# Attention scores from two fp16 parts on 32-row bands of TensorE, with the operand stacks loaded ahead of the row maxima

## What is computed

```python
q = (x @ Wq.T + bq).reshape(b, s, 16, 8)      # k and v in the same way
attn = jnp.einsum('bqhd,bkhd->bhqk', q, k) / np.sqrt(8)
attn = jax.nn.softmax(attn, axis=-1) * head_mask[None, :, None, None]
out = jnp.einsum('bhqk,bkhd->bqhd', attn, v).reshape(b, s, 128)
x = layernorm(x + out @ Wo.T + bo)
```

## Time and profile before

| | |
|---|---|
| median of 3 timed executions | 702.23 us (700.29 to 702.65) |
| span of the profiled execution | 760.8 us |
| PE busy | 489.5 us (64%) |
| DVE busy | 401.7 us (53%) |
| ACT busy | 307.2 us (40%) |
| POOL busy | 312.9 us (41%) |

### The profile page before, as it was taken

How to read it: one execution, slowest core, us unless ns; L and a number is a source line. 1 busy time by engine, 2 the same in 40 slices (tenths; PEclk the granted TensorE clock), 3 DMA queues, 4 the chain that set the end, 5 groups by cost and what they waited for, 6 DMA issues and landing times. The chain is left out here.

```text
span 760.8 us, 15877 instructions
## 1 busy us (share of the span) xinstructions
PE 489.5 (64%) x5002; PEld 345.1 (45%) x5003; DVE 401.7 (53%) x871; ACT 307.2 (40%) x551; POOL 312.9 (41%) x465
## 2 busy tenths in 40 slices
PE   2577777788776778876840510049959988989400
PEld 1244444455444445543440400049938877777300
DVE  3544545566454556645767200027737867777246
ACT  1044544554454555544634200027724434434115
POOL 7123333223333331321232777710004756666546
PEclk9879989999898998988975655559979989999755
DMA  2333335434443443453221111100092100000074
GB/s 78 95 97 90 87 99 135 115 100 125 114 134 83 135 120 100 120 150 100 65 72 48 50 53 53 53 12 0 0 241 61 32 29 31 31 30 31 16 202 130
DMA packets 86467, 63.05 MB, mean 83 GB/s; under 512 B 10982, under 2 KB 78896, under 8 KB 86432
## 3 DMA queue, kind: packets, MB, share of 16 engines
q1 hardware_dynamic: 81888, 54.13, 26.4%
q0 software_dynamic: 4544, 8.47, 3.4%
HBM read 31.65 MB, written 29.29 MB: 80 GB/s over the span
## 5 line engine op out<-in xcount | busy, mean ns | idle before, releaser
L456 DVE TENSOR_REDUCE row_max<-s_ps 128x2 f32<-128x512 f32 x256 | 163.9, 684 | 163.3 <-PE s_ps L533 162.0
L367 ACT ACTIVATE probs<-st_ps 128x1024 f32<-128x1024 f32 x128 | 129.3, 1024 | 112.9 <-PE st_ps L545 112.7
L533 PE MATMUL s_ps<-k_stack,q_stack 128*128 128x256 bf16 x512 | 109.6, 301 | 89.1 <-DMA k_stack<-k_rows 80.8
L1305 POOL DMA_INDIRECT results<-gated,dest x78 | 95.4, 1223 | 126.5 <-DVE gated L1408 101.8
L545 PE MATMUL st_ps<-q_stack,k_stack 128*128 128x256 bf16 x512 | 105.7, 293 | 1.2 <-ACT probs L367 1.2
L533 PEld LDWEIGHTS s_ps<-k_stack,q_stack 128*128 128x128 bf16 x512 | 39.8, 103 | 140.3 <-issue 60.3
L1379 ACT ACTIVATE hid_r<-h_ps_r,bias 128x256 f32<-128x256 f32 x156 | 61.2, 475 | 95.7 <-PE h_ps_r L901 54.1
L562 PE MATMUL av_ps<-probs,v_aug 128*32 128x256 f32 x1024 | 79.3, 434 | 0.2 <-ACT probs L367 0.2
L885 POOL DMA_INDIRECT slots<-rows,slot_at x64 | 62.1, 970 | 32.0 <-issue 18.9
L299 POOL TENSOR_SCALAR max_parts<-row_max 128x16 bf16<-128x16 f32 x32 | 6.6, 206 | 151.6 <-DVE row_max L456 149.3
L914 PE MATMUL y_ps_r<-w,hid_r 128*128 x312 | 61.0, 223 | 4.0 <-issue 4.0
(11 more groups left out here) (179 smaller groups left out, 1021.4 us busy)
## 6 DMA issues: line engine op xcount, KB each, us to landing
q_stack<-q_rows SPq DMA_DIRECT2D x32, 204.0 KB
k_rows<-qk_parts SPq DMA_DIRECT2D x96, 64.0 KB, 1.7
k_stack<-k_rows SPq DMA_DIRECT2D x32, 192.0 KB
slots<-empty_row SPq DMA_DIRECT2D x6, 780.0 KB, 10.2
expert<-results SPq DMA_DIRECT2D x16, 256.0 KB, 5.1
w_or_slots<-slots SPq DMA_DIRECT2D x3, 1040.0 KB, 12.0
q_rows<-qk_parts SPq DMA_DIRECT2D x16, 192.0 KB, 2.1
w_or_slots<-in_w_fc SPq DMA_DIRECT2D x9, 256.0 KB, 4.3
```

What stands on the lines that cost most here:

```text
L367: nc.scalar.activation(probs[:, p % 4], st_ps[:, p % 2], ACT.Exp, scale=SCORE_SCALE).then_inc(exp_done, 1)
L456: nc.vector.tensor_reduce(row_max[:, h], s1_ps[:, h % 2], AX_X, ALU.max, negate=True).then_inc(max_done, 1)
L533: mm = nc.tensor.matmul(s1_ps[:, h % 2, t], q_stack[:, b.par, h, t * P:(t + 1) * P], k_stack[:, b.par, h], start=True, stop=True)
L1305: nc.gpsimd.indirect_dma_start(out=a["results"][:, :], out_offset=bass.IndirectOffsetOnAxis(ap=dest[:, t.buf, half:half + 1], axis=0), in_ ...
```

## The change

q and k are split into two fp16 parts, so three products of parts give a score, with a contraction of 24 rows a head. The stacks hold four heads in each of four bands of 32 partitions; a matmul now takes a tile of 24 rows (26 for the shifted scores) of one band instead of 128. The maximum is scaled by 1/256 and split in two parts; k_stack is filled with 256 once, in place of ones and zeros, and stays so in the rows behind the 24. The zero rows of q_rows, the memset of q_stack and four DMAs at the start go. A slot now waits for everything first (wait_for_scores, wait_for_shifted) and then takes score and shifted score matmuls in turns; the shifted scores take the heads in the order n ^ 4, so that the two are always on different bands, and the quads follow in the order n ^ 1. In SP's queue the row writes are four DMAs instead of nine, a half of the stacks four instead of two, and load_max four instead of three; the first half of the stacks of `new` is issued ahead of load_max of `now`, the second half behind it.

```diff
@@ -22,7 +23,13 @@
-ROW_MAX = 6 * DH
+TERMS = 3
+BAND = 32
+BANDS = P // BAND
+IN_BAND = HEADS // BANDS
+TERM_ROWS = TERMS * DH
+MAX_PARTS = 2
+MAX_UNIT = 256.0
...
@@ -82,8 +89,8 @@
-        q_rows = nc.dram_tensor("q_rows", [2, ROW_MAX + 3, HEADS, SEQ], BF16, kind="Internal").ap()
-        k_rows = nc.dram_tensor("k_rows", [2, ROW_MAX, HEADS, SEQ], BF16, kind="Internal").ap()
+        q_rows = nc.dram_tensor("q_rows", [2, TERM_ROWS, HEADS, SEQ], F16, kind="Internal").ap()
+        k_rows = nc.dram_tensor("k_rows", [2, TERM_ROWS, HEADS, SEQ], F16, kind="Internal").ap()
@@ -111,15 +116,14 @@
-        qk_rest = sb("qk_rest", [D, 2, SEQ])
-        qk_parts = sb("qk_parts", [D, 2, 2, 3, SEQ], BF16)
-        q_stack = sb("q_stack", [P, 2, HEADS, SEQ], BF16)
-        k_stack = sb("k_stack", [P, 2, HEADS, SEQ], BF16)
+        qk_parts = sb("qk_parts", [D, 2, 2, 2, SEQ], F16)
+        q_stack = sb("q_stack", [P, 2, IN_BAND, SEQ], F16)
+        k_stack = sb("k_stack", [P, 2, IN_BAND, SEQ], F16)
...
@@ -199,29 +202,28 @@
-            sp.wait_ge(consts_made, 4)
-            for par in range(2):
-                sp.dma_start(q_rows[par, ROW_MAX:ROW_MAX + 3], zero_rows[:].unsqueeze(1).to_broadcast([3, HEADS, SEQ])).then_inc(zeros_out, 16)
-                sp.dma_start(k_stack[ROW_MAX:ROW_MAX + 3, par], one_rows[:].unsqueeze(1).to_broadcast([3, HEADS, SEQ])).then_inc(zeros_out, 16)
-            sp.wait_ge(zeros_out, 64)
-                for part in range(3):
-                    rows = HALF * TILES
-                    sp.dma_start(q_stack[ROW_MAX + part:ROW_MAX + part + 1, b.par, half * HALF:(half + 1) * HALF, :]
-                                 .rearrange("o h (t q) -> o (h t) q", t=TILES),
-                                 max_t[part * rows:(part + 1) * rows, half, :]).then_inc(max_in[half], 16)
+                rows = IN_BAND * TILES
+                for part in range(MAX_PARTS):
+                    for k in range(BANDS // 2):
+                        row = (half * (BANDS // 2) + k) * BAND + TERM_ROWS + part
+                        of = (part * (BANDS // 2) + k) * rows
+                        sp.dma_start(q_stack[row:row + 1, b.par].rearrange("o g (t q) -> o (g t) q", t=TILES),
+                                     max_t[of:of + rows, half, :]).then_inc(max_in[half], 16)
-                heads = slice(half * HALF, (half + 1) * HALF)
-                sp.dma_start(q_stack[0:ROW_MAX + 3, b.par, heads], q_rows[b.par, :, heads]).then_inc(stacks_in[b.par][half], 16)
-                sp.dma_start(k_stack[0:ROW_MAX, b.par, heads], k_rows[b.par, :, heads]).then_inc(stacks_in[b.par][half], 16)
+                for band in range(half * (BANDS // 2), (half + 1) * (BANDS // 2)):
+                    rows = slice(band * BAND, band * BAND + TERM_ROWS)
+                    heads = slice(band * IN_BAND, (band + 1) * IN_BAND)
+                    sp.dma_start(q_stack[rows, b.par], q_rows[b.par, :, heads]).then_inc(stacks_in[b.par][half], 16)
+                    sp.dma_start(k_stack[rows, b.par], k_rows[b.par, :, heads]).then_inc(stacks_in[b.par][half], 16)
...
@@ -243,31 +245,26 @@
-                    q_to = q_rows[b.par, 0:ROW_MAX].rearrange("(r d) h t -> (d h) r t", r=6)
-                    k_to = k_rows[b.par].rearrange("(r d) h t -> (d h) r t", r=6)
+                    q_to = q_rows[b.par].rearrange("(r d) h t -> (d h) r t", r=TERMS)
+                    k_to = k_rows[b.par].rearrange("(r d) h t -> (d h) r t", r=TERMS)
-                            sp.wait_ge(stacks_in[b.par][half], 32 * b.half)
-                    sp.wait_ge(qk_split, 4 * b.n + 1)
-                    for r in range(3):
-                        sp.dma_start(k_to[:, r:r + 1], k_part[:, 0:1]).then_inc(rows_out[b.par], 16)
-                    sp.wait_ge(qk_split, 4 * b.n + 3)
-                    for r in range(3, 5):
-                        sp.dma_start(k_to[:, r:r + 1], k_part[:, 1:2]).then_inc(rows_out[b.par], 16)
-                    sp.wait_ge(qk_split, 4 * b.n + 4)
-                    sp.dma_start(q_to[:, 0:3], q_part[:, 0:3]).then_inc(rows_out[b.par], 16)
-                    sp.dma_start(q_to[:, 3:5], q_part[:, 0:2]).then_inc(rows_out[b.par], 16)
-                    sp.dma_start(q_to[:, 5:6], q_part[:, 0:1]).then_inc(rows_out[b.par], 16)
-                    sp.dma_start(k_to[:, 5:6], k_part[:, 2:3]).then_inc(rows_out[b.par], 16)
-                b = Batch(u, c, 1)
-                if b.exists():
-                    load_max(b, 0)
-                b = Batch(u, c, 0)
-                if b.exists():
-                    sp.wait_ge(rows_out[b.par], 144 * (b.half + 1))
-                    load_stacks(b, 0)
-                    load_stacks(b, 1)
+                            sp.wait_ge(stacks_in[b.par][half], 64 * b.half)
+                    sp.wait_ge(qk_split, 2 * b.n + 1)
+                    sp.dma_start(q_to[:, 0:1], q_part[:, 0:1]).then_inc(rows_out[b.par], 16)
+                    sp.dma_start(k_to[:, 2:3], k_part[:, 0:1]).then_inc(rows_out[b.par], 16)
+                    sp.wait_ge(qk_split, 2 * b.n + 2)
+                    sp.dma_start(q_to[:, 1:3], q_part[:, 0:2]).then_inc(rows_out[b.par], 16)
+                    sp.dma_start(k_to[:, 0:2], k_part[:, 0:2]).then_inc(rows_out[b.par], 16)
+                new, now = Batch(u, c, 0), Batch(u, c, 1)
+                if new.exists():
+                    sp.wait_ge(rows_out[new.par], 64 * (new.half + 1))
+                    load_stacks(new, 0)
+                if now.exists():
+                    load_max(now, 0)
+                if new.exists():
+                    load_stacks(new, 1)
...
@@ -275,48 +272,38 @@
-            nc.gpsimd.memset(zero_rows[:], 0.0).then_inc(consts_made, 1)
-            nc.gpsimd.memset(one_rows[:], 1.0).then_inc(consts_made, 1)
...
-            nc.gpsimd.memset(q_stack[:].rearrange("p b h t -> p (b h t)").bitcast(F32), 0.0).then_inc(consts_made, 1)
...
-                    wait_first(pool, rows_out[b.par], 144 * b.half)
+                    wait_first(pool, rows_out[b.par], 64 * b.half)
-                pool.wait_ge(qk_split, 4 * b.n + 1)
-                nc.gpsimd.tensor_tensor(qk_rest[:], qk[:], parts[:, :, 0], ALU.subtract).then_inc(qk_split, 1)
-                wait_first(pool, qk_split, 4 * b.n + 2)
-                nc.gpsimd.tensor_scalar(parts[:, :, 1], qk_rest[:], 1.0, 1.0, ALU.mult, ALU.mult).then_inc(qk_split, 1)
-                pool.wait_ge(qk_split, 4 * b.n + 3)
-                nc.gpsimd.tensor_tensor(parts[:, :, 2], qk_rest[:], parts[:, :, 1], ALU.subtract).then_inc(qk_split, 1)
+                pool.wait_ge(qk_split, 2 * b.n + 1)
+                nc.gpsimd.tensor_tensor(parts[:, :, 1], qk[:], parts[:, :, 0], ALU.subtract).then_inc(qk_split, 1)
...
@@ -521,37 +508,49 @@
-                pe.wait_ge(consts_made, 7)
-            def scores(b, h):
+                pe.wait_ge(consts_made, 4)
+            def band_of(stack, b, h, rows):
+                lo = h // IN_BAND * BAND
+                return stack[lo:lo + rows, b.par, h % IN_BAND]
+            def wait_for_scores(b, h):
-                    pe.wait_ge(stacks_in[b.par][h // HALF], 32 * (b.half + 1))
+                    pe.wait_ge(stacks_in[b.par][h // HALF], 64 * (b.half + 1))
-                for t in range(TILES):
-                    mm = nc.tensor.matmul(s1_ps[:, h % 2, t], q_stack[:, b.par, h, t * P:(t + 1) * P], k_stack[:, b.par, h],
-                                          start=True, stop=True)
-                mm.then_inc(scores_ready, 1)
-            def shifted_scores(b, h):
-                p = h // 2
-                if h % HALF == 0:
-                    pe.wait_ge(max_in[h // HALF], 48 * (b.n + 1))
-                if h % 2 == 0 and (b.since(1) or p >= 2):
+            def scores(b, h, t):
+                mm = nc.tensor.matmul(s1_ps[:, h % 2, t], band_of(q_stack, b, h, TERM_ROWS)[:, t * P:(t + 1) * P],
+                                      band_of(k_stack, b, h, TERM_ROWS), start=True, stop=True)
+                if t == TILES - 1:
+                    mm.then_inc(scores_ready, 1)
+            def wait_for_shifted(b, n):
+                p = n // 2
+                if n % HALF == 0:
+                    pe.wait_ge(max_in[n // HALF], 64 * (b.n + 1))
+                if n % 2 == 0 and (b.since(1) or p >= 2):
-                for t in range(TILES):
-                    mm = nc.tensor.matmul(st_ps[:, p % 2, h % 2, t], k_stack[:, b.par, h, t * P:(t + 1) * P],
-                                          q_stack[:, b.par, h], start=True, stop=True)
-                if h % 2:
+            def shifted_scores(b, n, t):
+                p, h, rows = n // 2, n ^ 4, TERM_ROWS + MAX_PARTS
+                mm = nc.tensor.matmul(st_ps[:, p % 2, n % 2, t], band_of(k_stack, b, h, rows)[:, t * P:(t + 1) * P],
+                                      band_of(q_stack, b, h, rows), start=True, stop=True)
+                if n % 2 and t == TILES - 1:
-            def quad(b, g):
+            def quad(b, n):
```

(73 more changed lines are left out.)

4 lines of the change are left out of this document (2 added, 2 removed).

## The result

The changed kernel takes 657.62 us (median of 4, 650.02 to 659.51) against 701.99 us: a ratio of 0.934, 95% interval 0.928 to 0.940. It is faster by 44 us, where 79 (to 623) were forecast; the range ended at 655.

What follows compares the result with a forecast made beforehand. TensorE's wait for k_stack once a 22.09 us step was taken as the bound. Steps saved 85 us, start and step 1 14, together 99: span 760.8 to 662. Between 611 in proportion and 642, 623 us was chosen, range 598 to 655.

Steps and rivals of the forecast that it cites:

- (d): Score slots on row tiles: a slot's four matmuls take 0.3 us instead of 0.44, taking 0.3 us off a step.
- 16.0 us a step: Attention steps 2 to 15: forecast step time without the stall, against 22.09 us before, 85 us over 14 steps.
- the clock does not stay up: Rival, score slots: matmuls on 24 of 128 rows leave TensorE at 1.2 GHz; 714 us in proportion, chance 0.07.
- changes of shape: TensorE between tile shapes: about 0.1 us a change, 12 more changes a step, 1.2 us.
- first scores at 16: Start of the kernel: first scores near 16 us instead of 25.84, a gain of 9.8 us.
- (a): SP's queue: stacks ahead of the maxima and smaller, 192 KB a half; TensorE's 80.8 us wait for k_stack goes.
- (b): Maxima's rows queued behind the stacks: they land at 17.0, just in time for slot 0 at 17.3; at worst 1.5 us a step.
- The scaling to the median: Profiled span to timed median: the span's ratio of 0.870 applied to 702.23 us gives 611 us.
- the landings: DMA landings: were two thirds of the profiled run's extra 58.6 us there, the gain is 60 and the time 642 us.
- the reordering does nothing: Rival, stack loads: still late because the row writes are late; step near 20.5 us, 669 us, chance 0.09.
- The maxima's rows: Rival, slot 0: late maxima's rows take the stall's place; step of 18.5 us, 643 us in proportion, chance 0.19.

Runs made afterwards that it cites:

- one_band: full_rows with the score matmuls' operands cut to the 24 (26) rows that hold data, one behind another: 793.08 us, ratio 1.128.
- bands64: The changed kernel with two bands of 64 rows instead of four of 32, zeros below the 26 rows of data: 605.95 us, ratio 0.863.
- full_rows: The changed kernel without bands: one head on partitions 0 to 25, zeros below in q_stack, every score matmul on all 128 rows: 611.43 us, ratio 0.869.
- maxima_first: full_rows with SP's old order, the maxima's rows of the first half ahead of both halves of the stacks: 609.54 us, ratio 0.868.
- order_only: The kernel before with only the stacks' first half issued ahead of the maxima's rows: 656.45 us, ratio 0.9325.
- bands64_waits: bands64 with the shifted scores' wait moved behind the slot's first score matmul: 662.11 us, ratio 0.871, where the kernel before took 761.23 us.
- same_band64: bands64 with shifted scores in order n, a slot's four matmuls in one band: 680.56 us, ratio 0.894, where the kernel before took 761.23 us.

## Why the prediction was wrong

**The step that failed is (d), in what it left out**: the 16.0 us a step, priced at full clock, measured 18.87 us on average over six steps, with granted clocks from 0.54 to 1.00. With it failed the chance of the rival "the clock does not stay up". The prediction counted the row tiles' columns and changes of shape, and set the granted clock near 1.00 because before it fell only behind idle time. In the trace of before every matmul names 128 rows, so these rows could say nothing of matmuls on 24. The rival had the mechanism and was given 0.07; what was held against it, that the full-array work keeps coming, didn't help: in one_band it comes in every step too, at half clock. One of its prices holds: 27.6 us a step for half clock without overlap, and one_band takes 28.3. The other, 24 us with overlap, was too high: such a step of the change takes 22.1. The change itself is at half clock for part of the steps and at full clock for the others. Against a step of 15.87 in bands64, 18.87 is 3.0 more, times 14 = 42 us; that is the shortfall in the profiled execution, for bands64 ends attention 339.3 - 294.9 = 44.4 us earlier. The change's median is 7.6 us above its profiled execution, and 44.4 + 7.6 is the 52 us between the medians of the two.

**The sum for full clock was right.** 99 us were forecast; bands64 gains 391.6 - 294.9 = 96.7 by the end of attention. Its parts: first scores at 16, measured 15.62; a step of 16.0, measured 15.6 to 15.9 in the change at full clock and 15.87 in bands64; (a) no wait for k_stack beyond the first; (b) the maxima's rows in time, 2.7 us of waits in all, though their four issues take 2.71 and not 2.4 us; (d) pairs starting together, 0.22 us a slot rather than the 0.3 taken. What side by side running is worth was 0.3 us a step in the sum; full_rows against bands64 gives 16.47 - 15.87 = 0.6, and 5.5 us in time. About the changes of shape the prediction was right too: the quad at 143.51 starts 0.20 us behind the last pair where 0.11 is the rhythm, 0.09 us a change. The Trainium skill, TensorEngine Tiling (Array Packing), Key Properties, cited there, says that changing the tiling mode drains TensorE. The gap of 0.09 us agrees.

**(a) named the queue where size did most.** The place behind the maxima and the 792 KB in one go were treated as one cause. The runs part them: order alone 46 us, smaller stacks alone (maxima_first, which also has the shorter splits and start, and the matmuls in turns) 93, both (full_rows) 91.

**The scaling to the median was wrong.** The trace of before came from an execution 58.6 us slower than the median, and the prediction shared those between a proportion and the landings. They lie behind attention: from the first router matmul to the end it is 760.8 - 391.6 = 369 us there, 648.3 - 339.3 = 309 after the change and 309 in bands64, 308 in order_only, whose later stages are those of the kernel before, while bands64_waits, on the chip with 761 us for the kernel before, has 365. One row of its waits view:

```profile
ACT hid L1213 <- remote: 78.7, 3, 37.3
```

The same wait, 79.0 us, stands in the waits view of before, and none in those of the change and of bands64; what "remote" is, no view says. So the gain was to be subtracted, not scaled or cut: 702.2 - 99 = 603, and bands64 takes 606. The point chosen, 623, was nearer to the result only because two errors had opposite signs: the clock, which the sum left out, costs the change 657.6 - 606 = 52 us, and the unfounded choice had added 20. That part is luck.

Of the rivals, the one in which the reordering does nothing had the nearest number (669) and the wrong cause: order_only gains 46 us by it alone. The maxima's rows never took the stall's place (643).

## What to carry to other kernels

A tile of few rows may cost more than it saves, if TensorE's clock falls with it, as it did here: try the same matmuls with zero rows up to 64 or 128 before choosing the tile; here that won 52 us (64) and 46 us (128). When two cures for one stall come in one change (order and size here), price each alone. And find the place of a gap between a profiled execution and the median, in a stage the change doesn't touch or in one it does, before scaling by it.

## What the runs showed of the hardware

- With the same data, transfers and matmuls, 128 rows a matmul hold 2.4 GHz and 24 to 26 rows one behind another stay at 1.2 GHz through attention (611 and 793 us), while PE is busy all the time. With two 32-row tiles side by side the clock goes up and down, more up when all 32 rows are named (657.6 to 637.1 us). Two 64-row tiles side by side are at full clock but for the start and a stretch near 249 us (605.95 us), and one 64-row tile at a time from 50 us on (same_band64).
- The added rows add nothing to the result (zeros in q_stack against 256 in k_stack) and still keep the clock up. In the kernel before the rows behind the data are zeros in both stacks, and its quads away from a stall take 1.07 us.
- The clock column reads 1.00 for one_band's attention, where starts 0.21 us apart and a quad of 1.99 us say half, and 9 tenths at the start of the change, where the quads up to 44 us take 1.94. It can be trusted only where durations agree.
- Matmuls on different row tiles and different PSUM tiles start at the same time (143.19 and 143.19), each with its own weight load of 0.09 us.
